# Up product of a fused cross-attention and butterfly FFN kernel: seven Strassen block products over 1024 tokens, with split weights streamed from HBM

## The reference

```python
# gated scan, along the 512 steps of each sequence
r = 0.9 * r + ctx * ctx
x = x + layernorm(x) * r
# feed-forward
h = layernorm(x) @ W_exp + b_exp              # 512 -> 2048
h = gelu(butterfly(h, up_weights) + up_bias)  # 11 stages of 2x2 mixes
y = butterfly(h, down_weights) @ W_con + b_con + down_bias   # 2048 -> 512
out = x + y
```

## Time and profile before

| | |
|---|---|
| three runs, us | 2943.24 (median), 2942.32, 2948.14 |
| profiled execution | 2948.14 us, span of its instructions 2948.0 us |
| mean granted TensorE clock | 0.991 |
| TensorE / VectorE / ScalarE / GpSimd busy | 99% / 60% / 19% / 10% |
| moved by DMA | 148.75 MB, mean 50 GB/s |

### The profile page before, as it was taken

The page is one execution under the profiler, slowest core; times in us unless marked ns, Lnnn a source line. Parts: engine busy times, 40 slices in busy tenths (PEclk is TensorE's granted clock), DMA queues, the critical chain, the costliest instruction groups (busy, mean ns, idle before and its releaser), DMA issues.

```text
span 2948.0 us, 36069 instructions
## 1 busy us (share of the span) xinstructions
PE 2916.9 (99%) x13049; PEld 2414.5 (82%) x13049; DVE 1760.6 (60%) x3314; ACT 567.5 (19%) x788; POOL 289.9 (10%) x369
## 2 busy tenths in 40 slices
PE   7899999999999999999999999999999999999999
PEld 6778888888888888888888888888888888888887
DVE  6776555666555666655566655556665556665552
ACT  4721111111111111111111111111111111111111
POOL 4111001111001111100111100111110011110010
PEclk7999999999999999999999999999999999999999
DMA  9201221221221121222122122212112212212210
GB/s 200 52 15 48 58 58 29 57 49 37 57 57 45 41 57 39 47 57 57 31 55 51 36 56 57 49 37 57 39 47 57 57 33 53 54 34 55 57 29 15
DMA packets 141471, 148.75 MB, mean 50 GB/s; under 512 B 23772, under 2 KB 89404, under 8 KB 140860
## 3 DMA queue, kind: packets, MB, share of 16 engines
q1 hardware_dynamic: 136908, 147.19, 21.7%
q10 hardware_dynamic: 4464, 0.61, 0.2%
HBM read 80.63 MB, written 33.55 MB: 39 GB/s over the span
## 4 chain that ended last, share of the span: by engine, by line
PE 96%; SPq 1%; ACT 1%; DVE 0%; DMA 0%; issue 0%; DVEq 0%
PE ps L989 47%; PE ps L1000 47%; SPq L349 1%; ACT wexp L548 0%; ACT Z L548 0%; PE ps L905 0%; SPq L334 0%; DMA HX<-_L_ffn_down_weights_dram 0%; PE ps L916 0%; PE ps L926 0%; DVE W1lo L685 0%; PE ps L918 0%; ACT W1hi L544 0%; PE ps L960 0%; PE ps L866 0%
## 5 line engine op out<-in xcount | busy, mean ns | idle before, releaser
L820 DVE CAST ghi<-g 128x512 fp32r<-128x512 f32 x512 | 217.0, 424 | 1047.1 <-PE ps L1000 1042.9
L603 ACT ACTIVATE g<-ps,gelu_bias 128x512 f32<-128x512 f32 x512 | 354.1, 692 | 2301.8 <-PE ps L989 2268.5
L989 PE MATMUL ps<-xTlo,W1hi 128*128 128x512 f32 x2048 | 796.8, 389 | 0.3 <-DVE xThi L769 0.3
L1000 PE MATMUL ps<-W2hi,ghi 128*128 128x512 f32 x2048 | 796.7, 389 | 0.0
L1000 PE MATMUL ps<-W2lo,ghi 128*128 128x512 f32 x2048 | 796.7, 389 | 0.0
L989 PE MATMUL ps<-xThi,W1hi 128*128 128x512 f32 x2048 | 796.7, 389 | 0.0
L1000 PE MATMUL ps<-W2hi,glo 128*128 128x512 f32 x2048 | 796.7, 389 | 0.0
L989 PE MATMUL ps<-xThi,W1lo 128*128 128x512 f32 x1984 | 771.8, 389 | 0.0
L989 PEld LDWEIGHTS ps<-xTlo,W1hi 128*128 128x128 f32 x2048 | 384.5, 188 | 81.0 <-DVE xThi L769 1.1
L1000 PEld LDWEIGHTS ps<-W2hi,ghi 128*128 128x128 f32 x2048 | 384.8, 188 | 80.2
L1000 PEld LDWEIGHTS ps<-W2hi,glo 128*128 128x128 f32 x2048 | 384.3, 188 | 79.8
(11 more groups left out here) (109 smaller groups left out, 1392.8 us busy)
## 6 DMA issues: line engine op xcount, KB each, us to landing
kv<-in_ctx_dram SPq DMA_DIRECT2D x128, 256.0 KB, 4.3
x<-in_x_dram SPq DMA_DIRECT2D x128, 256.0 KB, 4.4
xTlo<-kv SPq DMA_DIRECT2D x496, 64.0 KB, 2.0
out_dram<-x SPq DMA_DIRECT2D x124, 256.0 KB, 4.0
wexp<-in_L_ffn_W_exp_dram SPq DMA_DIRECT2D x4, 1024.0 KB, 10.0
wcon<-in_L_ffn_W_con_dram SPq DMA_DIRECT2D x16, 256.0 KB, 11.0
Z<-in_L_ffn_up_weights_dram SPq DMA_DIRECT2D x1, 2048.0 KB, 19.2
wcon<-_L_ffn_down_weights_dram SPq DMA_DIRECT2D x1, 2048.0 KB, 15.1
```

The costliest lines, as they stand in the source:

```text
L603: act.activation(g32[:, k % 2, :].rearrange("p (j g i) -> p g j i", g=G, i=Q), ps_h[k % 2][:, :].rearrange("p (g j i) -> p g j i", g=G, i= ...
L820: nc.vector.tensor_copy(ghi[:, slot, :], g32[:, slot, :]).then_inc(ghi_ready, 1)
L989: last = nc.tensor.matmul(ps_h[k % 2][:, :], w, v, start=(i == 0), stop=(i == len(terms) - 1))
L1000: last = nc.tensor.matmul(ps_y[j][:, :], g[:, k % 2, tok], w[:, k, :], start=(k == 0 and i == 0), stop=(k == KH - 1 and i == 2))
```

## The change

**Turns of 1024 tokens.** The main part has U = 16 turns of two token halves, h = 0 (a) and h = 1 (b). For each of NP = 8 pairs p, the hidden chunks p and p + 8 are computed for both halves together. This is a 2x2 block product (two hidden chunks by two halves of the inputs, two token halves), done by Strassen's scheme in Winograd's form: seven products m = 0 to 6 of two 128-chunks each, 6 matmuls of 128x512 instead of 8 x 6. The sums of weight blocks are formed once (weight_sums on GpSimd), those of tokens once per turn (token_sums on GpSimd). Three of the sums of products are made by accumulating in PSUM, three with a copy of a bank to st by ScalarE (copy) and an add by VectorE (block_sum), which writes g32; the fourth result goes from PSUM to the gelu.

**Weights in HBM.** The operands of the seven products for all pairs (56 of 256 KB) and the split down weights (8 of 1 MB) no longer fit. They are split in the first part (weights_hi on ScalarE, weights_lo on VectorE), stored to HBM, and loaded again in every turn: refill loads product n + 8 when product n is done, into a ring of RING = 8 slots; load_w2 loads a pair's down weights one pair ahead.

**Down product.** down(u, p, h, j) is 6 matmuls: two hidden chunks, three terms, for 128 tokens. Half a is summed over all pairs in four banks, added to x by finish_a at the turn's end; half b has one bank, ps_yb, that add_b adds to x after each piece. The down pieces of the pair before stand between the products.

**Moved work.** Rounding the gelu (ghi) goes from VectorE to ScalarE; the add of the output bias goes to GpSimd (add_bias). The preparation of the next turn's two halves on VectorE is spread over the pairs: scan of a in pairs 0 and 1, statistics and gates of a in 2 (the last gate in 3), normalise in 3; scan of b in 4 (last chunk in 5), statistics and two gates in 5, the other gates and normalise in 6; tokens_lo of the next turn in 7, two of the seven in the next pair 0. In the first part the two halves of turn 0 are prepared before the main part starts, the second one between weights_lo(4) and weights_lo(7).

The diff, cut to its core (the new VectorE body is told above and stands here for pair 7 alone):

```diff
...
-    LAG = 2
-    KEEP_AT = (KH - 3, KH - 2)
+    U = T // 2
+    NP = KH // 2
+    NM = 7
+    RING = 8
+    PER = NP * NM
     NX = 16
     MOVES = G * G
-
+    XPOS = (0, 1, 5, 2, 3, 4, 6)
+    XORDER = (0, 1, 3, 4, 5, 2, 6)
+    W2SLOTS = 5
+    DN_ORDER = [k for p in range(NP) for k in (p, p + NP)]
...
+    w1_dram = nc.dram_tensor("w1_products", (PER, P, 4 * P), f32, kind="Internal").ap()
+    w2_dram = nc.dram_tensor("w2_split", (NP, P, 2, 2, D), f32, kind="Internal").ap()
...
+        ghi = sb("ghi", [P, 2, 4, J * P], f32r)
+        glo = sb("glo", [P, 2, 4, J * P], f32r)
+        raw = sb("raw", [P, 2, KD, J * P])
+        w1r = sb("w1r", [P, RING, 2, 2 * P], f32r)
+        w2r = sb("w2r", [P, 2, 2, 2, D], f32r)
+        g32 = sb("g32", [P, 4, J * P])
+        st = sb("st", [P, 3, J * P])
...
+        xop = sb("xop", [P, NM, 2, 2, J * P], f32r)
...
+            def move_xT(u, h):
+                sp.wait_ge(xn_turned, u * (2 * J) + (h + 1) * J)
                 for q in range(G):
                     for g in range(G):
...
+                        sp.dma_start(raw[Q * q:Q * q + Q, h, :, g * P:(g + 1) * P],
+                                     turned[Q * g:Q * g + Q, :, q, :]).then_inc(xT_moved[h], NX)
...
+            def load_ctx(u, h):
+                if h:
+                    sp.wait_ge(xT_moved[0], (u + 1) * (MOVES * NX))
                 else:
...
+                    wait(sp, xT_moved[1], u * (MOVES * NX))
+                load_tokens(kv, 0, ctx_rows, u * 2 + h, ctx_loaded)
...
+            for p in range(NP):
+                for m in range(NM):
+                    n = p * NM + m
+                    sp.wait_ge(w1_lo, n + 1)
+                    sp.dma_start(w1_dram[n], w1r[:, n % RING, :, :].rearrange("p a n -> p (a n)").bitcast(f32))\
+                      .then_inc(w1_stored[n % RING], NX)
+                if p == 2:
+                    sp.wait_ge(fold_made, fold_at("regroup", 0) + 1)
+                    move_xT(0, 0)
+                if p == 3:
+                    load_ctx(0, 1)
+            for n in range(RING):
+                sp.wait_ge(w1_stored[n], PER // RING * NX)
+                load_w1(n, n)
+            move_xT(0, 1)
...
+            for s in range(W2SLOTS):
+                sp.wait_ge(w2_stored[s], len(range(s, KH, W2SLOTS)) * NX)
+            load_w2(0)
+            load_w2(1)
+            def refill(u, p, m, last):
+                n = p * NM + m + RING
+                if last and n >= PER:
+                    return
+                sp.wait_ge(m_done, u * PER + (p * NM + m + 1))
+                load_w1(n % PER, n % RING)
...
+            def body(u, par, first, last):
+                for p in range(NP):
+                    if p == 0 and not last:
+                        load_ctx(u + 1, 0)
+                    for m in range(NM):
+                        refill(u, p, m, last)
+                        if p == 1 and m == 1 and not first:
+                            store(u - 1, 1 - par)
+                        if p == 1 and m == 3 and not last:
+                            load_x(u + 1, 1 - par)
+                        if p == 4 and m == 0 and not last:
+                            load_ctx(u + 1, 1)
+                    if p == 3 and not last:
+                        sp.wait_ge(xlo_ready, (u + 1) * NM)
+                        move_xT(u + 1, 0)
+                    if p == 6 and not last:
+                        move_xT(u + 1, 1)
+                    if not (first and p == 0) and not (last and p >= NP - 1):
+                        sp.wait_ge(d_done, u * (NP * 2 * J) + p * (2 * J))
+                        load_w2((p + 1) % NP)
...
+            def add_bias(t, h, x):
+                for j in range(J):
+                    pool.wait_ge(xn_ready, t * J + (j + 1))
...
+                wait(pool, w1_lo, p * NM)
+                nc.gpsimd.tensor_tensor(out=s1, in0=a21, in1=a22, op=ALU.add).then_inc(wsum_ready, 1)
...
+                pool.wait_ge(xT_moved[1], (u + 1) * (MOVES * NX))
+                pool.wait_ge(xlo_ready, u * NM + 1)
+                nc.gpsimd.tensor_tensor(out=r11, in0=r12, in1=r11, op=ALU.subtract).then_inc(xsum_ready, 1)
+                pool.wait_ge(xsum_ready, u * 4 + 1)
+                nc.gpsimd.tensor_tensor(out=r12, in0=r22, in1=r12, op=ALU.subtract).then_inc(xsum_ready, 1)
...
+            for p in range(3, 7):
+                weight_sums(p)
+            rstd(1)
+            weight_sums(7)
+            add_bias(1, 1, xs[0])
+            token_sums(0)
+            def body(u, x):
+                for h in range(2):
+                    rstd(u * 2 + h)
+                    add_bias(u * 2 + h, h, x)
+                token_sums(u)
...
+            weights_hi(0)
+            for q in range(R // 4):
+                fold_step("turn_high", q)
+            act.wait_ge(bias_low, 1)
+            act.activation(yb, ps[3][:, 256:256 + KH], ACT.Copy).then_inc(yb_kept, 1)
+            weights_hi(1)
+            for r in range(R // 2):
+                fold_step("high_dn", r)
+            weights_hi(2)
+            for r in range(R // 2, R):
+                fold_step("high_dn", r)
+            weights_hi(3)
+            for q in range(KH // 4):
+                fold_step("turn_low", q)
             for k in range(KH):
...
+                fold_step("back", k)
+            weights_hi(4)
...
+                for p in range(NP):
+                    ahead = p == NP - 1 and not last
+                    if p == 0 and not first:
+                        tokens_hi(u, 2, False)
+                    if p == 4 and not last:
+                        square(u * 2 + 3)
+                    copy(p, 0, ps_b, 0)
+                    if ahead:
+                        tokens_hi(u + 1, 0, False)
+                    gelu(p, 0, 0, p)
+                    if ahead:
+                        tokens_hi(u + 1, 1, False)
+                    copy(p, 1, ps_b, 2)
+                    if p == 0 and not first:
+                        tokens_hi(u, 6, False)
+                    copy(p, 2, ps_c, 3)
+                    if p == 0 and not last:
+                        square(u * 2 + 2)
+                    if ahead:
+                        tokens_hi(u + 1, 3, False)
+                    gelu(p, 1, 1, p + NP)
+                    if ahead:
+                        tokens_hi(u + 1, 4, False)
+                    gelu(p, 2, 2, p)
+                    if ahead:
+                        tokens_hi(u + 1, 5, False)
+                    gelu(p, 3, 3, p + NP)
...
+                def block_sum(p, n, bank, i, m):
+                    q = (0, 1, 2)[n]
+                    dve.wait_ge(m_done, u * PER + (p * NM + m + 1))
+                    dve.wait_ge(copied, u * (NP * 3) + (p * 3 + i + 1))
+                    if not (first and p == 0):
+                        dve.wait_ge(glo_ready, u * (NP * 4) + ((p - 1) * 4 + q + 1))
...
+                    if go and p == 7:
+                        tokens_lo(u + 1, 0)
+                        tokens_lo(u + 1, 1)
...
+                    later_b(p, 1)
+                    low_part(p, 0)
...
+                    if go and p == 7:
+                        tokens_lo(u + 1, 3)
+                    block_sum(p, 1, ps_b, 2, 4)
+                    later_b(p, 2)
+                    low_part(p, 1)
...
+                        tokens_lo(u + 1, 4)
+                    block_sum(p, 2, ps_c, 1, 5)
+                    if old:
+                        finish_a(u - 1, nxt, 2)
+                    if go and p == 7:
+                        tokens_lo(u + 1, 5)
+                    low_part(p, 2)
+                    later_b(p, 3)
+                    low_part(p, 3)
...
+            def product(u, p, m, first):
+                n = p * NM + m
+                slot = n % RING
+                if p == 0:
+                    pe.wait_ge(xlo_ready, u * NM + (XPOS[m] + 1))
+                pe.wait_ge(w1_loaded[slot], u * (PER // RING * NX) + (n // RING + 1) * NX)
+                if m == 0 and not (first and p == 0):
+                    pe.wait_ge(gelu_ready, u * (NP * 4) + p * 4)
+                if m == 2:
+                    pe.wait_ge(copied, u * (NP * 3) + (p * 3 + 1))
+                if m == 4:
+                    pe.wait_ge(copied, u * (NP * 3) + (p * 3 + 2))
+                if m == 5:
+                    pe.wait_ge(copied, u * (NP * 3) + (p * 3 + 3))
+                if m == 6:
+                    pe.wait_ge(h_ready, u * (NP * 3) + (p * 3 + 2))
+                bank = (ps_b, ps_a, ps_b, ps_c, ps_b, ps_c, ps_b)[m]
+                opens = m in (0, 1, 3)
+                terms = [(w, v, c) for c in range(2) for w, v in ((0, 0), (0, 1), (1, 0))]
+                for i, (w, v, c) in enumerate(terms):
+                    last = nc.tensor.matmul(bank[:, :], w1r[:, slot, w, c * P:(c + 1) * P], xop[:, XPOS[m], v, c, :],
+                                            start=(opens and i == 0), stop=(i == len(terms) - 1), skip_group_check=True)
```

(78 more changed lines are left out.)

600 lines of the change are left out of this document (351 added, 249 removed).

## The result

The changed kernel takes **3338.1 us** (median of 4 runs, 3329.3 to 3342.9) against 2942.8 us (2941.4 to 2948.1): ratio 1.134, 95% interval 1.132 to 1.136. The forecast had the sign and the two long stops of a turn, but 3221 us is 117 us short, and the range ended at 3310. The change removed its 768 matmuls and TensorE still lost 395 us.

The account below looks back on a forecast made before the run. TensorE, busy 99%, bounds the kernel. 2948.0 - 174.1 (matmuls) + 352.5 (stops in 15 turns) + 90 (prologue) + 10 (first pair, tail) = 3226 us, median 4.9 lower: 3221 us; range 3065 to 3310 us.

Parts of the forecast that it names:

- 768 matmuls, 174.1 us: Main part: 48 fewer matmuls in each of 16 turns, at 0.2267 us each, save 174.1 us.
- VectorE per pair under 20.4 us: Each pair of a turn: VectorE's work sums to 12.8 to 17.5 us, under TensorE's 20.4 us.
- Pair 4's stop, 16 us: Before product 2, TensorE waits for copy, square, context load: 16 us (13.1 to 17); E is pair 3's end.
- The clock after it, 2.5 us: Behind the stop in pair 4, TensorE runs at a slow clock: 2.5 us lost per turn, low end 1.7.
- Pair 7, 4 us: Turn's end: token sums and splits delay gelu 3 and the next turn's first product by 4 us (0.3 to 5.5).
- The clock behind the turn's end: Start of the next turn: the prediction had no such term, charging a slow clock only behind pair 4's stop.
- Small waits, 1 us, bound 1.5: Pairs 0, 5 and 6: long pieces ahead of block sum 2 cost 1 us per turn (0 to 1.5).
- Prologue, 90 us: Before the first product: weight splits, waits, second token block, stores and token splits add 90 us (65 to 115).
- First pair 4 us, tail the rest of 10: First pair without down pieces to cover its chain, 4 us; with the longer last store together 10 us (5 to 16).
- Covered: Rival, pair 4's product 2: context lands before TensorE stops, pair 7 at its low end; 2844 us, chance 0.06.
- the weight stream: Rival, every turn: reloading weights and tokens at 150 GB/s takes 210 us a turn; 3617 us, chance 0.04.
- The port binds: Rival, every turn: each GpSimd hold of VectorE ends on the path, 240 us more; 3461 us, chance 0.08.

Follow-up runs that it names:

- run 5: The changed kernel with half b's context loaded early into a place of its own and the token splits moved behind block sums and gelus: 2930.5 us.
- run 7: The changed kernel with GpSimd's four token sums formed over an eighth of the columns, splits in their old place: 3252.8 us.
- run 4: The changed kernel with the weights' reloads cut to 16 of 128 partitions: 3282.0 us.
- run 3: The changed kernel with half b's context load put ahead of the weight loads in SP's queue: 3292.0 us.
- run 10: The same kernel as run 5, timed in 11 runs: 2936.9 us, ratio 0.998 to the kernel before the change.
- run 11: The kernel of run 10 with the second token block prepared earlier in the prologue: 2927.0 us, ratio 0.994 to the kernel before the change.

## Why the prediction was wrong, step by step

Two steps failed in the turns: no slow clock was charged behind the stop at the turn's end (35 us in all), and the small waits were taken at 1 us per turn and measured 4.2 (48 us). A third, the first pair, was taken at 4 us and measured 21.4.

- **768 matmuls, 174.1 us**: right. 5376 + 4096 + 2048 matmuls of the main part are 11520, and where nothing waits a product with its down piece still takes 2.72 us.
- **VectorE per pair under 20.4 us**: right. It was busy 14.6 to 17.8 us of a pair (means over 14 turns), and never bound by its sum.
- **Pair 4's stop, 16 us**: 17.0. The chain was right link by link. The landing was at the high end (whose terms, E+9, 10.3, 1.9 and 0.65 less 5.4, add to 16.4 and not to the 17 of the text), and the moves, for which the text had no upper bound, took up to 11.5 us.
- **The clock after it, 2.5 us**: 2.2 to 2.3 (12 matmuls in 5.0 us instead of 2.72).
- **Pair 7, 4 us**: 4.76. GpSimd's sums take 2.4 to 2.7 us, not the 2.0 from the 2048 row.
- **The clock behind the turn's end: missing, 2.35 us.** This is the step that failed as a step. The text charged the clock to the long stop alone, though its own rows show it behind a gap of 3.13 us; the stop of 4 us that it forecast was longer than that one and should have got the same term: 35 us in 15 turns.
- **Small waits, 1 us, bound 1.5**: 30.7 - 17.0 - 2.3 - 4.8 - 2.35 = 4.2 us, mis-sized the most. They lie in all eight pairs, 0.1 to 1.0 us each, where the text had looked at pairs 0, 5 and 6 alone. The end of pair 4 shows how one comes about:

```profile
943.71 0.70 DVE L895 STREAM_TRANSPOSE kv<-kvT 128x512 f32<-128x512 f32 x1
944.34 0.65 DVE L1025 TENSOR_TENSOR g<-ps,st 128x512 f32<-128x512 f32 x1
...
947.04 1.19 PE L1272 MATMUL ps<-xop,w1r 128*128 128x512 f32 x4 [0.43 <-ACT g L755]
```

Block sum 2 stands behind a scan chunk that runs from 941.40, gelus 2 and 3 behind block sum 2, and the next product behind gelu 3. GpSimd does nothing beside it, so this is a long piece ahead of a block sum and not a hold. These waits at the ends of pairs 4, 5 and 6 are the same in runs 5 and 7. The other small waits were not separated.

- **Prologue, 90 us**: the first product starts at 235.6 us, in the forecast window of 235 to 255, 78.4 us later than before (157.17). Some 12 us high: "back" ended at 159 instead of 167, low_dn at 234 instead of 243.
- **First pair 4 us, tail the rest of 10**: the first pair takes 30.9 us for 42 matmuls that need 9.5, so 21.4 us of waits, since GpSimd's four sums begin only at 235.7, when the first split is made, and the splits and the first copy stand behind them. The text charged "seven token splits" (8 us) to the prologue, where they do not stand before the first product, and forgot the sums they wait for. Prologue and first pair together took 99.8 us, where the text had 94. The tail costs 4.4 more (10.2 us from the first store's issue to the end, before 5.8).

The sum with measured terms: -174.1 + 15 x 30.7 + 78.4 + 21.4 + 4.4 = 390.6 us; the two spans differ by 387.5. Of the 117 us missed, 15 x 7.2 = 108 are the turns, mostly the second clock term (35) and the small waits (48).

The rivals: *Covered* and *the weight stream* are refuted by the stop itself and by run 4. *The port binds*, in its strong form of 240 us, fails (VectorE's longest splits cost 5.7 us per turn with the wait for the sums together, run 7), but its mechanism is a part of pair 7's stop; how large a part, run 7 does not separate. The text argued against it with 2.9 us of room in the fullest pair, though by its own holds pair 6 rose to 20.4 and had none.

The Trainium skill (TensorE: Matmul & The Clock Gate, What's actually happening), as the prediction cited it, holds the array at 1.2 GHz after idling; both windows above agree, 0.52 and 0.57. The Trainium skill (SBUF — State Buffer, SBUF: two separate sides) speaks of an exclusive lock between GpSimd and a VectorE operation with two SBUF inputs: the splits of 2.76 and 3.37 us beside the sums agree, and run 7, with short sums, has them back at 1.23.

## What to carry to other kernels

Fewer matmuls pay only as far as the engines' handovers stay hidden: here 11 us saved per turn were bought with two chains, each of which ends on TensorE. Where an instruction that feeds TensorE stands in a queue behind one that waits for a DMA, work out the whole chain, move, load, first user, and give the load a buffer of its own or a place pairs earlier; both fixes here are changes of order and place that cost no work, and turned 395 us of loss into 5 us of gain, 18 with the prologue reordered. When a stop is forecast, look in the rows for how short a gap was already followed by the slow clock, and charge it behind every such stop, not only the longest: here it followed the stops of 17 and 4.8 us in every turn, and those of some 2 us in run 5 only now and then (granted clock 0.66 in 1408.5 to 1413.5 us behind 2.35 us, 1.00 in 1075 to 1080 behind 2.09). Work out the longest pieces ahead of each sum that feeds TensorE, pair by pair, and for a step that is to be moved earlier look first at what that step itself waits for.

## What the runs showed of the hardware that was not expected

- The sixteen 64 KB moves hold SP's queue 10.3 us in pair 6, in every turn, as before, and 10.3 to 11.5 us in pair 3. With the weights' reload cut to an eighth (run 4) they still take 10.3 to 11.7 us there, so it is not the weights that stretch them. What does was not found.
- A context load landed 4.7 us after its last issue with the weights behind it or cut to an eighth (runs 3 and 4), and 7.8 us with 1.3 MB of weights issued in the 1.3 us before it.
- GpSimd's sum of 1024 columns takes 2.35 us alone (244.92 in run 5), 2.4 or 2.7 us in the turns, and 3.2 us where a split of VectorE already runs (235.66 and 245.96 in the first pair): the hold works in both directions.
- With the large stop at the turn's end gone, another appears at each return of the loop: TensorE and ScalarE stand still for some 2 us and wait for nothing that the view names (TensorE 1.8 to 2.4 us, six times each in runs 5, 10 and 11).
